# Block 0's first layer tile by tile, the small half of a weight split on GpSimd, and two groups of step 0 in another place

## What is computed

```
for i in range(3):                      # F0 = 39, S = 128
    Wr = Ws[i].reshape(F0, Fk, S)       # Fk = 39, 64, 64
    out = relu(einsum('bfd,bgd,fgs->bsd', x, h, Wr) + b[i])
    if i != 2:
        h, direct = out[:, :S // 2], out[:, S // 2:]
    else:
        direct = out
    outs.append(direct)
result = sum(concatenate(outs, axis=1), axis=-1)    # 512 x 256
```

## Time and profile before

| | us |
|---|---|
| median of 3 runs | 569.29 |
| lowest, highest | 567.89, 571.07 |
| the profiled execution | 568.57 |
| its span in the trace | 566.7 |
| PE, DVE, POOL, ACT busy in the span | 552.3, 535.1, 508.9, 386.8 |

### The profile page before, as it was taken

The page is one execution under the profiler, slowest core; times in us unless marked ns, Lnnn a source line. Parts: engine busy times, 40 slices in busy tenths (PEclk is TensorE's granted clock), DMA queues, the critical chain, the costliest instruction groups (busy, mean ns, idle before and its releaser), DMA issues.

```text
span 566.7 us, 7925 instructions
## 1 busy us (share of the span) xinstructions
PE 552.3 (97%) x2039; PEld 384.9 (68%) x2039; DVE 535.1 (94%) x488; ACT 386.8 (68%) x444; POOL 508.9 (90%) x225
## 2 busy tenths in 40 slices
PE   7699999999999999999999999999999999999997
PEld 4365667667677776777777676767767777677765
DVE  5858999999999999999999999999999999999975
ACT  1445787775867777585866867677686777858563
POOL 1565999999999999999999999999999999999995
PEclk9979999999999999999999999999999999999999
DMA  8996944918467392855829276491946649163001
GB/s 323 410 414 243 405 162 142 368 57 328 183 202 281 121 357 80 297 222 164 317 97 357 101 256 246 144 354 63 351 141 232 249 135 380 43 220 111 2 0 38
DMA packets 29844, 121.76 MB, mean 215 GB/s; under 512 B 3584, under 2 KB 3712, under 8 KB 27776
## 3 DMA queue, kind: packets, MB, share of 16 engines
q1 hardware_dynamic: 29824, 121.52, 58.9%
HBM read 120.98 MB, written 0.52 MB: 214 GB/s over the span
## 4 chain that ended last, share of the span: by engine, by line
PE 85%; POOL 4%; DVE 4%; issue 4%; DMA 1%; ACT 1%; SPq 0%; POOLq 0%; DVEq 0%; ACTq 0%
PE acc L636 85%; POOL z_lo L309 4%; DVE z_raw L454 1%; DVE z_whole L454 1%; DMA xfirst<-x 1%; DVE z_psum L454 1%; DVE w_hi L519 0%; DVE z_lo L309 0%; ACT h L727 0%; ACT z_hi L724 0%; SPq L318 0%; DVE sums L486 0%; POOL squares L580 0%; DVE sums L470 0%; SPq L344 0%
## 5 line engine op out<-in xcount | busy, mean ns | idle before, releaser
L309 POOL TENSOR_TENSOR z_lo<-z_raw,z_hi 128x1024 fp32r<-128x1024 f32 x202 | 478.4, 2406 | 33.3 <-ACT z_hi L724 33.1
L724 ACT CAST z_hi<-z_raw 128x1024 fp32r<-128x1024 f32 x202 | 208.8, 1047 | 92.7 <-DVE z_raw L454 87.5
L454 DVE TENSOR_TENSOR z_raw<-h,xwide 128x1024 f32<-128x1024 f32 x187 | 222.8, 1212 | 3.8 <-ACT h L727 3.7
L636 PE MATMUL acc<-z_hi,w_hi 128*128 128x512 f32 x560 | 202.9, 443 | 6.2 <-DVE w_hi L519 6.2
L636 PE MATMUL acc<-z_lo,w_hi 128*128 128x512 f32 x560 | 177.4, 398 | 1.4 <-POOL z_lo L309 1.3
L636 PE MATMUL acc<-z_hi,w_lo 128*128 128x512 f32 x528 | 169.4, 397 | 0.0
L636 PEld LDWEIGHTS acc<-z_hi,w_hi 128*128 128x128 f32 x560 | 105.8, 189 | 60.2 <-issue 34.0
L636 PEld LDWEIGHTS acc<-z_lo,w_hi 128*128 128x128 f32 x560 | 104.1, 188 | 30.1 <-POOL z_lo L309 5.8
L636 PE MATMUL acc<-z_whole,w_whole 128*128 128x512 f32 x256 | 120.0, 592 | 0.4 <-DVE z_whole L454 0.4
L636 PEld LDWEIGHTS acc<-z_hi,w_lo 128*128 128x128 f32 x528 | 99.6, 189 | 24.2
L309 DVE TENSOR_TENSOR z_lo<-z_psum,z_hi 128x1024 fp32r<-128x1024 f32 x78 | 94.7, 1214 | 1.8 <-ACT z_hi L724 1.1
(11 more groups left out here) (35 smaller groups left out, 157.6 us busy)
## 6 DMA issues: line engine op xcount, KB each, us to landing
xwide<-x SPq DMA_DIRECT2D x160, 512.0 KB, 4.9
xfirst<-x SPq DMA_DIRECT2D x14, 1792.0 KB, 8.6
xfirst<-x SPq DMA_DIRECT2D x16, 256.0 KB, 8.7
xfirst<-x SPq DMA_DIRECT2D x4, 512.0 KB, 11.5
xwide<-w SPq DMA_DIRECT2D x2, 1024.0 KB, 14.0
xfirst<-x SPq DMA_DIRECT2D x2, 768.0 KB, 10.1
w_whole<-w_whole SPq DMA_DIRECT2D x2, 256.0 KB, 12.7
z_raw<-w0c SPq DMA_DIRECT2D x1, 384.0 KB, 6.7
```

The lines of the kernel that those rows point to most:

```text
L309: return eng.tensor_tensor(lo[:, 0:n, :], z[:, 0:n, :], hi[:, 0:n, :].bitcast(F32), ALU.subtract)
L454: nc.vector.tensor_tensor(dst, in0, in1, ALU.mult).then_inc(made[kind], 1)
L636: return nc.tensor.matmul(dst, weights, z[0:rows, t - G * g, :], start=first and first_g and t == G * g, stop=final and t == TILES[layer] - 1)
L724: nc.scalar.copy(z_hi[0:rows, slot("PV", pair, par, pos, HI_RING), 0:n, :], src).then_inc(hi_made, 1)
```

## The change

Layer 0 of block 0 is done tile by tile: seven transfers (the first with slots 0 and 1, then one slot each) with a semaphore each, seven products of 128x512 with the three additions of weights between them, and PE waits for half a group. The bias now comes after all of x, and the list of loads ahead of `xwide` grows from eight to eleven. `WARM` goes from 12 to 10.

The small part of layer 1's low weights is taken from DVE's step 0 and made by POOL ahead of the large part, with a wait of POOL on its own result between the two. ACT rounds the weights of layer 1 before it writes `direct`, no longer after.

In step 0 group 7 of layer 1 stands fourth instead of eighth, and group 8 is W instead of P.

```
-ORDER_0 = "11W 13W 10W 12V 16P 14W 15P 17W 18P 19V 00W 01P 02W 03S"
+ORDER_0 = "11W 13W 10W 17W 12V 16P 14W 15P 18W 19V 00W 01P 02W 03S"
-UNDER1_AT, UNDER2_AT = (0, 8), (1, 6)
+UNDER2_AT = (1, 6)
-WARM = 12
+WARM = 10
...
-            load_first(0, xfirst_head_in[0], range(0, 1 + G))
+            load_first(0, xtile_in[0], range(0, 2))
             sp.dma_start(w0_part[0], w0a).then_inc(w0_in[0], 16)
+            load_first(0, xtile_in[1], [2])
             sp.dma_start(w0_part[1], w0b).then_inc(w0_in[1], 16)
-            load_first(0, xfirst_head_in[1], range(1 + G, 1 + 2 * G))
+            load_first(0, xtile_in[2], [3])
+            load_first(0, xtile_in[3], [4])
             sp.dma_start(w0_part[2], w0c).then_inc(w0_in[2], 16)
+            for t in range(2 * G, T0):
+                load_first(0, xtile_in[t], [1 + t])
             sp.dma_start(bias[:], b).then_inc(bias_in, 16)
-            load_first(0, xfirst_in, range(1 + 2 * G, T0))
-            load_first(0, xlast_in, range(T0, 1 + T0))
...
-            sp.wait_ge(whole_used, before("W", 0, 8))
+            sp.wait_ge(whole_used, before("W", 0, 9))
...
+            def first_product(t):
+                g = t // G
+                rows = rows_of(0, t)
+                dve.wait_ge(xtile_in[t], 16)
+                other = xshift[0:rows, t, :]
+                dst = z_whole[0:rows, slot("W", -1, 0, g, WHOLE_RING), t - G * g, :]
+                nc.vector.tensor_tensor(dst, other if t == T0 - 1 else xfirst[0:rows, 0, :], other, ALU.mult).then_inc(
+                    made["W"] if t == tiles_of(0, g)[-1] else first_half_made, 1)
...
-                    if isinstance(j, int) and (j, pos) == UNDER1_AT:
-                        split_under(1, w1_lo_made, len(SPLIT0) + 1)
...
-            products(-1, 0, 0)
+            first_product(0)
             fold(0)
+            first_product(1)
             fold(1)
-            products(-1, 0, 1)
+            first_product(2)
+            first_product(3)
             fold(2)
-            for pos in range(2, len(order(-1))):
-                products(-1, 0, pos)
+            for t in FOLD[2]:
+                first_product(t)
...
+            n = SPLIT_COUNT[1] - 1
+            pool.wait_ge(w_hi_made, len(SPLIT0) + 1)
+            pool.wait_ge(w_lo_made, len(SPLIT0) - 1)
+            nc.gpsimd.tensor_tensor(w_hi[HALF:, SPLIT_FROM[1] + n, :], stage[1][HALF:, n, :],
+                                    w_hi[HALF:, SPLIT_FROM[1] + n, :].bitcast(F32), ALU.subtract).then_inc(w1_lo_made, 1)
+            pool.wait_ge(w1_lo_made, 1)
             split_layer(1, len(SPLIT0) + 1).then_inc(w1_lo_made, 1)
...
                     for t in ts:
+                        if isinstance(j, int) and j < 0:
+                            if t == ts[-1]:
+                                pe.wait_ge(made["W"], number + 1)
+                            else:
+                                pe.wait_ge(first_half_made, g + 1)
                         mm = matmul(w, z, t, True, True)
...
                 relu(h[0][HALF:, :], a[0:HALF, :], 0, slice(0, HALF)).then_inc(h_ready[0], 1)
+                if isinstance(j, int) and j < 0:
+                    split_layer(1)
                 relu(direct[HALF:, half, :], a[HALF:, :], 0, slice(HALF, SIZE)).then_inc(acc_read[0], 1)
...
             relu0(-1, 0)
-            split_layer(1)
```

More of the change, by code:

```diff
@@ L245, in cin @@
         xfirst_in = sem("xfirst_in")
-        xlast_in = sem("xlast_in")
+        xtile_in = [sem(f"xtile_in{t}") for t in range(T0)]
+        first_half_made = sem("first_half_made")
         xfirst_head_in = [sem("xfirst_head_in0"), sem("xfirst_head_in1")]
@@ L404, in products @@
                 if layer == 0:
[L405 to L413, removed]
+                    if isinstance(j, int) and j == 0:
                         if g == 0:
@@ L416, in products @@
                         if g < len(xfirst_head_in):
-                            dve.wait_ge(xfirst_head_in[g], 32)
+                            dve.wait_ge(xfirst_head_in[g], 16)
                         else:
-                            dve.wait_ge(xfirst_in, 32)
+                            dve.wait_ge(xfirst_in, 16)
                     elif g == 0:
                         dve.wait_ge(xrep_ready, j + 1)
[L422 to L426, removed]
+                        dve.wait_ge(xfirst_in, 16 * (j + 1))
+                    in0 = xrep_psum[0:rows, None, :].to_broadcast([rows, n, N])
                     in1 = xshift[0:rows, G * g:G * g + n, :]
-                    if g == len(KINDS[0]) - 1:
-                        in0 = in1
                 elif layer == 1:
@@ L647, in contract @@
                 if kind == "W":
-                    pe.wait_ge(made["W"], number + 1)
+                    if not isinstance(j, int) or j >= 0:
+                        pe.wait_ge(made["W"], number + 1)
                     z = z_whole[:, slot("W", pair, par, pos, WHOLE_RING)]
@@ L741, in copy_xrep @@
                 if isinstance(j, int) and j == 0:
-                    act.wait_ge(xfirst_head_in[0], 32)
+                    act.wait_ge(xfirst_head_in[0], 16)
                 else:
-                    act.wait_ge(xfirst_in, 16 * (j + 2))
+                    act.wait_ge(xfirst_in, 16 * (j + 1))
                 if not isinstance(j, int) or j > 0:
```

## The result

| | before | after |
|---|---|---|
| median of 7 runs each | 569.29 | 566.03 |
| lowest, highest | 567.89, 571.07 | 565.42, 566.92 |
| the profiled execution | 568.57 | 566.03 |
| its span | 566.7 | 563.9 |
| mean granted clock of PE in it | 0.994 | 0.999 |

The ratio of after to before is 0.994, 95% interval 0.9921 to 0.996: 3.3 us or 0.6% faster. The forecast was 563.2, its range 561.8 to 566.8. The time lies in the range, 2.8 us above the forecast and above the forecast's own range (562.2 to 564.2). It is near that of rival B (565.4), and the traces show why: B came true, and layer 2's weights landed later than forecast.

A forecast was written before the change was run, and what follows sets the result against it. PE bounds the long middle, reached through the chain DVE starts with 10P in step 1. 10P starting at 42.8 instead of 48.88 gives 6.1 us: 569.29 - 6.1 = 563.2, range 561.8 to 566.8 (forecast's own 562.2 to 564.2).

The forecast's parts named there:

- rival B: DVE's small part in step 1 gets locked out behind POOL's `z_lo`, losing 2.2 us after 10P: 565.4; chance 0.32.
- 10P earlier: DVE's product for the first split group of step 1 starts at 42.8 instead of 48.88: 6.1 us, the whole gain.
- Step -1: Tile-by-tile products end at 12.9 to 13.3 instead of 13.42; relu starts 0.7 to 1.1 us earlier, at 14.3 to 14.7.
- Where that goes: DVE's 10W in step 0 waits for group 0 of `xwide` until 18.35, against 18.97 before; 0.6 us left on DVE.
- The small part and the fourth W: Step 0: POOL's small part takes 0.4 us, its large part ends at 23.8; PE's 6.19 us idle and half clock go.
- What is late next: Step 1: layer 2's weights land unmoved at 34.95, ACT rounds from 35.0, DVE's products start at 38.2, 10P at 42.8.
- C: PE's wait is replaced by later landings or a clock drop at another gap: 567; chance 0.14.
- D: Slower: work in single tiles and shorter `WARM` leave PE at half clock until 36: 572.3; chance 0.03.
- PE's further 1.5 us come back as waits for POOL.: PE starts step 1 7.6 us earlier, but 1.5 us return as waits for POOL's `z_lo` in steps 1 and 2.

The follow-up runs named there:

- small_alone: no_tiles with step 0's group order (and SP's wait at eight W groups) as in the kernel before; 562.72 us, ratio 0.9894 to the kernel before.
- relu_first: no_tiles with ACT's relu of layer 1 ahead of the rounding of layer 2's weights in step 1; 562.16 us, ratio 0.9885.
- small_relu: Kernel before plus layer 1's small part on POOL, ACT's new order, layer 2's small part one product earlier, relu ahead of rounding in step 1; 562.19 us.
- u2_early: Changed kernel with layer 2's small part on DVE one product earlier in step 1, behind 10P instead of 11W; 564.07 us, ratio 0.9932.
- first_three: u2_early with slots 0 to 2 (768 KB) in block 0's first transfer again, the rest tile by tile; 563.2 us, ratio 0.9921.
- after_again: The changed kernel unaltered, in 9 more runs on another chip; 565.6 us, ratio 0.9942 to the kernel before.
- no_tiles_late: no_tiles with layer 2's small part back in its old place behind 11W in step 1; 564.88 us, ratio 0.9918.
- before_no_lock: Kernel before with both small parts on DVE one product earlier, ahead of the W product, nothing else; 564.65 us, ratio 0.994.
- no_tiles: u2_early without the tile-by-tile part: step -1, its loads and `WARM` as in the kernel before; 562.68 us, ratio 0.9909.

## Why the prediction was right and wrong

Right in its mechanism: PE bounds the middle, PE's start of step 1 (6.88 us earlier) is not the gain, and DVE's 10P and what follows it is. The four places of the accounting, in us of the profiled executions:

| | forecast | measured |
|---|---|---|
| 10P earlier | 6.1 | 5.36 |
| lost in the lock after it | 0 (rival B: 2.2) | 2.22 |
| left at 23P, the product behind the lock | 6.1 | 51.58 - 48.43 = 3.15 |
| more idle time of DVE before 00V | 0 | 0.55 - 0.14 = 0.41 |
| left at 00V | 6.1 | 60.32 - 57.59 = 2.73 |
| span | 6.1 | 566.7 - 563.9 = 2.8 |

(51.58 and 60.32 are the starts of 23P and 00V in the kernel before.)

In these executions the forecast is missed by 3.3 us. By the medians it is 2.8, for the median of before lies 0.72 above its profiled execution. That the time lies in the stated range is owed to B, which the range took in; what the forecast itself said, 6.1 us, came to 2.8 in the spans. It is partly luck: the late landing and the idle time before 00V (0.74 + 0.41 us) stood neither in the forecast nor in B, and most of them is hidden by those 0.72.

**Step -1.** Relu at 14.65, forecast 14.3 to 14.7: right. But the last tile was made at 11.39 + 1.97 = 13.36, not at 12.9 to 13.3, and before it was 13.43; the 0.7 us came from PE alone, which had only the last records behind it. And the term "the first of them about 0.6 us earlier (256 KB less in front, at the 422 GB/s of the earlier trace rows)" failed: the transfer of 512 KB took 4.7 us from issue to landing, that of 768 KB 4.6. A rate of a full queue was put on a queue that had just begun; in the fourth microsecond it moved 236 GB/s.

**Where that goes.** "So of this part 0.6 us are left on DVE" failed with it. The weights of layer 1 released ACT at 17.82 (17.0 forecast), group 0 of `xwide` released DVE for 10W at 19.10 (18.35 forecast): everything behind the start is some 0.75 us late. Before, DVE had come to 10W at 18.97 by its own pace, so that nothing of the 0.6 is left. The earlier relu was swallowed by a DMA wait of 0.74.

**The small part and the fourth W.** Right: POOL's small part took 0.45 (0.4 forecast), PE waits 0.22 us, and the clock is 1.00 throughout. POOL's large part ended at 24.58 instead of 23.8, the landing again; PE had the cover, for its own work was late by the same. small_alone shows that the fourth W was not needed for it.

**What is late next.** The place was right, ACT's rounding of layer 2's weights; the term "the bytes ahead of them are the same, so this does not move" was mis-sized: 35.69 for 35.0. The bytes are the same but not the time that the first ones take. Without the tiles the rounding started at 34.93 and the forecast of 42.8 for 10P met 42.76.

**The choice between forecast and B.** This is the larger error, 2.2 of the 3.3 us. The mechanism stood in the prediction with place and price, and the price was right (2.2 forecast, 2.22 measured). But B had 0.32 against 0.46. With two earlier cases, one each way, and starts 0.01 us apart, a half was the least that the rows bore out; 13 of 16 runs fell on the long side. The median of such a kernel is that of the more frequent side.
By what the Trainium skill says in "SBUF — State Buffer", section "SBUF: two separate sides", the pair is held for a whole instruction and the other engine fully blocks.
The traces agree: a DVE small part that was locked out ended 0.15 or 0.16 us after POOL's instruction, every time. But the prediction drew too much from it with "can't cost something in between". That is so where both start together (0.29, or 2.48 to 2.51). In relu_first and small_relu, where DVE came near the end of a POOL instruction, it paid the rest of that one and took 0.48 and 0.50.

**Rivals C and D.** D fell: no window from 20 to 40 is under 1.00. C is half right: the landing did come 0.7 us late, but no second stretch at the lower clock replaced the first.

**PE's waits.** "PE's further 1.5 us come back as waits for POOL." PE's waits over 0.15 us from 45 to 80 (waited for: us in total, times, longest us), in the changed kernel and then in u2_early:

```profile
PE acc L647 <- POOL z_lo L311: 3.4, 4, 1.2
```

```profile
PE acc L647 <- POOL z_lo L311: 1.8, 3, 0.8
```

The kernel before has none in this window. Without the lock 1.8 us come back, near the forecast's 1.5; the lock adds 1.6.

**Left open.** The 0.41 us more before 00V. The row names DVE's own `z_lo`, which is the instruction ahead, as its releaser. The idle time stands in the changed kernel, u2_early, first_three and after_again, all with the tile part, and in none without it; it keeps its place in the program when the time of that place moves. Which wait of DVE it is, and why the tiles bring it, no run shows.

## What to carry to other kernels

A small instruction that can be locked out belongs where its neighbour on the other engine surely isn't, not 0.01 us beside it: moving the two small parts by one place was worth about as much here (3.2 us) as the whole change (3.3). Before a transfer is cut to land its first piece earlier, look at what the queue moves in its first microseconds, not at its full rate. And test each part of a change alone: here one part gave the gain, one nothing that can be measured, and one took 1.4 us back.

## What was not expected of the hardware

- DVE and POOL that start within 0.01 us of one another are a toss over runs of one program: by their spans 13 of 16 runs of the changed kernel and 4 of 6 of no_tiles_late lost 2.2 us, the rest nothing, and the recorded order of the starts (45.41 and 45.42, DVE free) does not tell which.
- At the start of the program, 256 KB less in the first transfer bring nothing: 4.7 us against 4.6, with 236 against 362 GB/s in the fourth microsecond at nearly the same busy share.
- A DVE instruction that comes late in a POOL instruction pays only what is left of it: 0.48 us in relu_first, where POOL had 0.32 us to go, against 2.50 when both start together.
- Runs of the kernel before spread over 5.9 us (565.68 to 571.55, 16 runs on the first chip), those of before_no_lock over 3.2 (8 runs, of which three kept the full clock), those of no_tiles over 0.6 (6 runs). PE's idle time at the start of step 0 falls in the same order (6.19 us, 2.87, none), and so does the stretch at 0.50. But the clock is not all of it: ten of the 16 runs of before have the same mean clock, 0.994, and lie between 566.87 and 571.55. Both small parts of that kernel start within 0.01 us of POOL, so two tosses of 2.2 us may stand in its spread as well, and before_no_lock removes both. How much is due to each no run shows.
